# A two-layer graph network on one core: diagonal blocks written by twelve small DMAs a graph instead of one GpSimd product, and the order of steps laid out anew

## The chip, the core and the metric

The kernel runs on one core of a Trainium2 chip. Five engines work side by side, each through its own list of instructions: TensorE (PE in the profile, its weight loads PEld), VectorE (DVE), ScalarE (ACT), GpSimd (POOL) and SyncE (SP), which here only issues DMAs. They wait for one another by semaphores. The metric is the device time of one launch, in microseconds (us), lower is better.

## The reference

64 graphs of 128 nodes and 384 features, with a 128x128 adjacency matrix each. Layer 0 is masked attention with 6 heads of 64, a residual and a layer norm. Layer 1 is graph attention with 12 heads of 32:

```python
h = jnp.einsum('bnd,ade->bane', feat_in, W)
th = jnp.tanh(h)
attn_src = jnp.einsum('bane,aeo->bano', th, w_src)
attn_dst = jnp.einsum('bane,aeo->bano', th, w_dst)
attn = attn_src + jnp.swapaxes(attn_dst, 2, 3)
attn = jnp.where(attn >= 0, attn, LEAKY_ALPHA * attn)
attn = jnp.where(mask, jnp.float32(-999.0), attn)
attn = jax.nn.softmax(attn, axis=-1)
feat_out = jnp.einsum('banm,bame->bane', attn, h) + b
...
feat_out = jax.nn.elu(feat_out)
gate = jax.nn.sigmoid(feat_in @ H_w.T + H_b)
return gate * feat_out + (1.0 - gate) * feat_in
```

Then a second residual and layer norm.

## The kernel before

The 64 graphs go through in 16 groups of 4. Each engine runs the same frame (`phases`): a phase "load", a phase "first" (layer 0 of group 0), "second" (one pass of the loop order, for group 0), a loop of 13 passes, "drain" (a pass without the loads) and "last" (layer 1 of the last group). A pass of the loop order does layer 1 of group u, layer 0 of group u+1 and the transposes of x of group u+2. Inside a phase the order of every engine is a table written out by hand: `PE_LOOP`, `ACT_LOOP`, `DVE_LOOP`, `POOL_LOOP` and so on, of steps (name, graph or part). An engine works through its table in that order and waits at a step until its operands are there.

The large projections (steps v, qk, h, gate, f; line L480) are split into a high and a low part, so each is nine matmuls into one of two PSUM banks `p_bank`. Transposes and the step wb use two banks `t_bank`. A bank is free when ACT and DVE have read it.

The attention weights of layer 1 need, for each of the 12 heads, the outer combination of a value a source node and a value a destination node. The way there, for graph k of a group, is this chain:

- h (PE), th (ACT, hout), prod (POOL, L1020), sd (DVE, L895), sda (DVE, L902: a 128x24 addition in SBUF), pqw and qwhi (ACT), qwlo (DVE), qwT (PE, L610: transpose to 96 rows), qwTo (ACT, L760: copy to SBUF).
- rows (POOL, L1027): `w_rows` holds for each head n a 96x128 block in which only rows n, 32+n and 64+n are kept. It is one product of `qwT`, repeated 12 times along the free dimension, with the 0/1 mask `own_head`.
- wb (PE, L619): three matmuls of 512 columns (4 heads each) of `qwT` with `w_rows`. Then e (DVE, L924: four instructions a step) makes the weights and pv1 (PE, L630) applies them to h.

`w_rows` has two buffers, by k % 2. After pv1 come rden1, f_raw (DVE), fb (POOL), elu (ACT), ex (POOL), mixa (DVE, L942: both inputs in SBUF), mixb, sum1, stats1, mv1, rstd1, out and the store. The step x_res (POOL, L1003) adds a bias to the four graphs of x at once. In layer 0, pv0 (L564) is followed by chi (ACT) and clo (DVE), which free the operand of f.

In "first", DVE's step consts (L784 to L792) prepares small constants and waits for the last of the weight DMAs; PE's step ob multiplies two biases.

SP issues, in each pass, the load of x and adj of group u+2, and then the four stores of group u, each after its step out.

Of the kernel before, what the change touches and what calls it, by code (L numbers as in the profile page):

```python
# [1088 lines left out]
```

## Time and profile before

| what | value |
|---|---|
| time, median of 3 runs | 1256.72 us (1253.74 to 1256.73) |
| span of the profiled execution, first to last instruction | 1255.7 us |
| TensorE busy | 1134.4 us, 90% |
| VectorE busy | 1000.4 us, 80% |
| GpSimd busy | 697.6 us, 56% |
| ScalarE busy | 624.8 us, 50% |
| one pass of the loop | 75.1 us |
| mean granted TensorE clock | 0.960 of full speed |

The profiled execution has no other time than its span; the median of the runs lies 1.0 us above it. A pass of the loop repeats from pass to pass, so one is read for all. Durations of instructions that are pipelined overlap: the distance from one start to the next is what a piece takes from its engine. A busy share says how full an engine is; what a stage waits for is in the brackets of the timeline, which name the idle time before a piece and what ended it.

### The profile page before, as it was taken

Reading aid. Unit: us, or ns where it says so; the run is one execution under the profiler, and the core shown is the slowest. Engines: PE = TensorE matmul, PEld = TensorE weight load, DVE = VectorE, ACT = ScalarE, POOL = GpSimd, SP = SyncE. Lnnn points to the kernel's source line nnn. Section 1 sums busy time; section 2 is a strip of 40 time slices with the busy share of each in tenths; the row PEclk is TensorE's granted clock in tenths of the full one; section 3 lists DMA queues with packets and bytes.
Section 4 is the critical chain, followed back from the end, with each engine's and each line's share of the span. In section 5 each row is a group of like instructions: output and inputs, shape, how many; then the busy total and the mean of one; then the engine's idle time right before and its main releaser. Section 6 shows DMA issues by size and latency. Waiting matters only on the chain.

```text
span 1255.7 us, 25554 instructions
## 1 busy us (share of the span) xinstructions
PE 1134.4 (90%) x7791; PEld 1006.7 (80%) x7791; DVE 1000.4 (80%) x2384; ACT 624.8 (50%) x1996; POOL 697.6 (56%) x605
## 2 busy tenths in 40 slices
PE   6999999989899998999989899998999989899885
PEld 4888888878888887888878888887888878788774
DVE  4769789696987969788797987969788797987857
ACT  4645464454635545464554635545464554635422
POOL 0346565564655656565565655656565565656544
PEclk9998999999999999999999999999999999999975
DMA  6100010001000010010101000010010001000000
GB/s 166 29 28 8 20 29 26 27 6 28 24 19 27 13 40 6 19 33 19 27 13 39 7 19 27 13 40 6 19 33 19 27 13 40 6 19 2 26 1 26
DMA packets 34719, 30.95 MB, mean 25 GB/s; under 512 B 15872, under 2 KB 34688, under 8 KB 34688
## 3 DMA queue, kind: packets, MB, share of 16 engines
q1 hardware_dynamic: 34688, 30.57, 8.0%
q8 instruction: 16, 0.26, 0.1%
q14 instruction: 15, 0.12, 0.0%
...
## 4 chain that ended last, share of the span: by engine, by line
PE 55%; issue 16%; DVE 14%; POOL 9%; ACT 5%; DMA 0%; ACTq 0%; POOLq 0%; DVEq 0%; SPq 0%
PE p_bank L480 36%; PE context L630 7%; PE t_bank L619 4%; POOL w_rows L1027 4%; PE context L564 3%; DVE sda L902 3%; DVE weights L924 2%; POOL prod L1020 2%; PE t_bank L512 2%; PE t_bank L590 2%; POOL elu_steps L1038 1%; POOL f_b L1032 1%; ACT x1T L720 1%; DVE sd L895 1%; DVE neg_max L842 1%
## 5 line engine op out<-in xcount | busy, mean ns | idle before, releaser
L924 DVE SCALAR_TENSOR_TENSOR weights<-t_bank,pqw,clip 128x128 f32<-128x128 f32 x768 | 212.8, 341 | 33.6 <-PE t_bank L619 32.3
L1027 POOL TENSOR_TENSOR w_rows<-qwT,own_head 96x1536 fp32r<-96x1536 f32 x64 | 176.1, 2752 | 68.2 <-ACT qwT L760 68.2
L630 PEld LDWEIGHTS context<-h,weights 128*128 128x128 f32 x1536 | 197.3, 199 | 10.9 <-DVE weights L924 5.4
L630 PE MATMUL context<-h,weights 128*128 128x33 f32 x1536 | 193.0, 275 | 3.8 <-DVE weights L924 3.8
L1020 POOL TENSOR_TENSOR prod<-th,w_sd 128x768 f32<-128x768 f32 x64 | 117.6, 1838 | 132.6 <-ACT th L727 132.6
L699 ACT ACTIVATE probs<-masked,neg_max 128x128 f32<-128x128 f32 x384 | 148.8, 390 | 39.7 <-DVE neg_max L842 39.6
L1008 POOL TENSOR_TENSOR probs<-probs,rden 128x768 f32<-128x768 f32 x64 | 99.8, 1559 | 101.6 <-DVE rden L847 101.6
L480 PE MATMUL p_bank<-w_f,cT 128*128 128x384 f32 x576 | 125.8, 366 | 22.3 <-DVE cT L795 22.2
L480 PEld LDWEIGHTS p_bank<-w_f,cT 128*128 128x128 f32 x576 | 104.1, 199 | 29.4 <-DVE cT L795 29.3
L480 PE MATMUL p_bank<-w_h,x1T 128*128 128x384 f32 x576 | 117.7, 349 | 1.7 <-DVE x1T L795 1.7
L480 PE MATMUL p_bank<-w_g,x1T 128*128 128x384 f32 x576 | 117.0, 349 | 0.0
L480 PE MATMUL p_bank<-w_v,xT 128*128 128x384 f32 x576 | 116.7, 347 | 0.0
L480 PE MATMUL p_bank<-xT,w_q 128*128 128x512 f32 x432 | 112.2, 405 | 3.2 <-DVE w_k L804 3.0
L1038 POOL TENSOR_TENSOR elu_steps<-elu_steps,x 128x384 f32<-128x384 f32 x64 | 64.6, 1010 | 89.1 <-ACT elu_steps L771 89.0
L619 PE MATMUL t_bank<-w_rows,qwT 96*128 96x512 f32 x192 | 82.9, 473 | 29.6 <-POOL w_rows L1027 19.6
L480 PE MATMUL p_bank<-xT,w_k 128*128 128x512 f32 x432 | 109.0, 397 | 0.0
L480 PEld LDWEIGHTS p_bank<-w_g,x1T 128*128 128x128 f32 x576 | 104.8, 194 | 4.8 <-issue 2.6
L480 PEld LDWEIGHTS p_bank<-w_h,x1T 128*128 128x128 f32 x576 | 101.0, 193 | 2.9 <-DVE x1T L795 2.2
L480 PEld LDWEIGHTS p_bank<-w_v,xT 128*128 128x128 f32 x576 | 100.2, 190 | 1.1 <-issue 0.2
L480 PEld LDWEIGHTS p_bank<-xT,w_k 128*128 128x128 f32 x432 | 81.6, 189 | 20.0
L480 PEld LDWEIGHTS p_bank<-xT,w_q 128*128 128x128 f32 x432 | 80.8, 191 | 19.7 <-DVE w_k L804 3.4
L1032 POOL TENSOR_TENSOR f_b<-f_raw,bias 128x384 f32<-128x384 f32 x64 | 67.1, 1048 | 51.8 <-DVE f_raw L935 51.8
...
## 6 DMA issues: line engine op xcount, KB each, us to landing
...
out_dram<-y_out SPq DMA_DIRECT2D x64, 192.0 KB, 1.9
...
x<-in_L_gnn_W_dram SPq DMA_DIRECT2D x3, 192.0 KB, 6.0
```

Source lines behind the costliest of these rows:

```text
L480: last = te.matmul(dst, left(a, kt), right(b, kt), start=(n == 0), stop=(n == 3 * KT - 1))
L564: last = te.matmul(context0[b * HD0:(b + 1) * HD0, j * P:(j + 1) * P], v[:, k, n * HD0:(n + 1) * HD0], probs0T[:, k % 2, b, j * P:(j + 1) ...
L619: te.matmul(dst[:, :], qwT[:, g % 2, 0, :], w_rows[0:QW_ROWS, g % 2, heads, :].rearrange("p h i -> p (h i)"), start=True, stop=True).then_ ...
L630: last = te.matmul(context1[:, n * (HD1 + 1):(n + 1) * (HD1 + 1)], weights[:, n, :], h[:, g % 2, n, :], start=True, stop=True)
L699: last = act.activation(probs0[:, k % 2, b, j * P:(j + 1) * P], masked[:, k % 2, b * PAIRS + j, :], ACT.Exp, bias=neg_max[:, b * PAIRS + j ...
L902: dve.tensor_tensor(sda[:], sd[:], sd_shift[:], ALU.add).then_inc(s_sda, 1)
L924: last = dve.scalar_tensor_tensor(out=weights[:, n, :], in0=src[:, i * P:(i + 1) * P], scalar=pqw[:, g % 2, 0, n:n + 1], in1=clip[:, g, :] ...
L1008: pool.tensor_tensor(probs, probs, per_head(rden0[:], P), ALU.mult).then_inc(s_norm, 1)
L1020: pool.tensor_tensor(prod[:], over_heads(th[:], 2), w_sd[:], ALU.mult).then_inc(s_prod, 1)
L1027: pool.tensor_tensor(w_rows[0:QW_ROWS, k % 2], over_heads(qwT[:, k % 2, 1, :].bitcast(F32), H1), per_head(own_head[:], P), ALU.mult).then_ ...
L1032: pool.tensor_tensor(f_b[:, k % 2, :].rearrange("p (h e) -> p h e", h=H1), f_raw[:].rearrange("p (h e) -> p h e", h=H1), over_heads(bias_1 ...
L1038: pool.tensor_tensor(exp_less_x, f_exp, x1[:, k, :], ALU.subtract).then_inc(s_ex, 1)
```

## The change

The product on GpSimd, its mask and the lines that made the mask are gone. `w_rows` is set to zero once. Then SP issues for each graph twelve DMAs from SBUF to SBUF; each copies one head's three rows of 128 values from `qwT` into `w_rows`. SP's program is no longer a straight list but a table of steps like the others. PE waits for the full count of the twelve DMAs on one of two semaphores. PE's steps v and gate have each one wait more (for x's and x1's low part). All tables are written anew; a line of them stands for the rest.

```diff
-    ("prod", 0), ("x_res", 0), ("prod", 1), ("rows", 0), ("rows", 1), ("norm", 0), ("prod", 2), ("fb", 0),
...
+    ("prod", 0), ("prod", 1), ("norm", 0), ("x_res", 0), ("fb", 0), ("prod", 2), ("ex", 0), ("norm", 1), ("prod", 3),
...
+SP_LOOP = [
+    ("rows", 0), ("rows", 1), ("load", 0), ("rows", 2), ("rows", 3), ("store", 0), ("store", 1), ("store", 2),
+    ("store", 3),
+]
...
+                elif name == "rows":
+
+                    if phase == "second" and k == 0:
+                        sp.wait_ge(s_zeroed, 1)
+                        sp.sem_inc(s_rows_free, 1)
+                    sp.wait_ge(s_qwT, upto(g1, GROUP, k + 1))
+                    sp.sem_inc(s_rows_free, 1)
+
+                    wait(sp, pe["wb"], upto(g1, THIRDS * GROUP, THIRDS * (k - 1)))
+                    sp.sem_inc(s_rows_free, 1)
+                    for n in range(H1):
+                        sp.dma_start(w_rows[n:QW_ROWS:BLOCK, k % 2, n, :].bitcast(F32),
+                                     qwT[n:QW_ROWS:BLOCK, k % 2, 1, :].bitcast(F32)).then_inc(s_rows[k % 2], 16)
...
-                    te.wait_ge(s_rows, upto(g1, GROUP, g + 1))
+                    te.wait_ge(s_rows[g % 2], upto(g1, ROWS_A_GROUP, (g // 2 + 1) * ROWS_A_GRAPH))
...
-                elif name == "rows":
-                    pool.wait_ge(s_qwT, upto(g1, GROUP, k + 1))
-
-                    wait(pool, pe["wb"], upto(g1, THIRDS * GROUP, THIRDS * (k - 1)))
-                    if phase == "second" and k == 0:
-                        pool.wait_ge(s_head, 4)
-                    pool.tensor_tensor(w_rows[0:QW_ROWS, k % 2], over_heads(qwT[:, k % 2, 1, :].bitcast(F32), H1),
-                                       per_head(own_head[:], P), ALU.mult).then_inc(s_rows, 1)
```

In "first" the tables of PE and DVE now begin so:

```diff
-    ("qk", 0), ("qk", 1), ("qk", 2), ("qk", 3), ("maskT", 0), ("qk", 4), ("qk", 5), ("ob", 0), ("s", 0),
+    ("ob", 0), ("qk", 0), ("qk", 1), ("qk", 2), ("qk", 3), ("maskT", 0), ("qk", 4), ("qk", 5), ("s", 0), ("v", 0),
...
-    ("qklo", 0), ("qklo", 1), ("consts", 0), ("qklo", 2), ("qklo", 3), ("wlo", 2), ("qklo", 4), ("wlo", 3),
+    ("consts", 0), ("wlo", 2), ("qklo", 0), ("wlo", 3), ("qklo", 1), ("qklo", 2), ("clip", 0), ("qklo", 3),
```

GpSimd at the start of the loop, before. L1020 is prod, L1003 x_res, L1027 rows, L1008 norm; the lines without operands are register work.

```order
L1020 TENSOR_TENSOR prod<-th,w_sd 128x768 [waits sd_made,th_made]
L997 ISA
L360 REGISTER_ALU [waits x_loaded]
L1003 TENSOR_TENSOR x_res<-x_in,out_bias 128x1536 [waits sum0_made]
L1015 REGISTER_ALU
L1020 TENSOR_TENSOR prod<-th,w_sd 128x768 [waits sd_made,th_made]
L360 ISA [waits qwT_copied]
L1027 TENSOR_TENSOR w_rows<-qwT,own_head 96x1536 [waits pe_wb]
L1027 TENSOR_TENSOR w_rows<-qwT,own_head 96x1536 [waits pe_wb,qwT_copied]
L1006 REGISTER_ALU
L1008 TENSOR_TENSOR probs<-probs,rden 128x768 [waits rden0_made]
```

The same place now; L1025 is prod, L1013 norm, L1008 x_res, L1029 fb.

```order
L1025 TENSOR_TENSOR prod<-th,w_sd 128x768 [waits sd_made,th_made]
L1020 REGISTER_ALU
L1025 TENSOR_TENSOR prod<-th,w_sd 128x768 [waits sd_made,th_made]
L1011 ISA
L1013 TENSOR_TENSOR probs<-probs,rden 128x768 [waits rden0_made]
L1002 ISA
L1008 TENSOR_TENSOR x_res<-x_in,out_bias 128x1536 [waits sum0_made,x_loaded]
L379 REGISTER_ALU [waits f_made]
L1029 TENSOR_TENSOR f_b<-f_raw,bias 128x384 [waits mixb_made]
```

The two products w_rows have left this stretch, and x_res stands behind prod of graph 1 and norm of graph 0.

SP in the loop, before; L426 and L427 load x and adj, L433 stores.

```order
L426 ISA [waits adj_b_made,pe_xT,x_res_made]
L426 DMA x_in<-in_x_dram 128x4x384
L427 REGISTER_ALU
L427 DMA adj_in<-in_adj_dram 128x4x128
L432 ISA
L433 ISA [waits y_made]
L433 DMA out_dram<-y_out 128x384
```

SP in the loop now, up to the last of the row DMAs (L442); the four stores follow.

```order
L442 DMA w_rows<-qwT 3x128 [waits pe_wb]
L442 DMA w_rows<-qwT 3x128 x11
L436 REGISTER_ALU
L442 DMA w_rows<-qwT 3x128 [waits qwT_copied,pe_wb]
L442 DMA w_rows<-qwT 3x128 x11
L425 ISA
L429 ISA [waits adj_b_made,pe_xT,x_res_made]
L429 DMA x_in<-in_x_dram 128x4x384
L430 REGISTER_ALU
L430 DMA adj_in<-in_adj_dram 128x4x128
...
L442 DMA w_rows<-qwT 3x128 [waits pe_wb]
L442 DMA w_rows<-qwT 3x128 x11
```

The rows of graphs 0 and 1 stand ahead of the load, those of graphs 2 and 3 behind it and ahead of the stores; between the eleven DMAs of a run there is no other instruction.

PE around the transpose of graph 3 (L610 before, L619 now), before: L564 is pv0, L480 a projection, L552 pT, L630 pv1, L619 wb.

```order
L610 MATMUL t_bank<-ident,qw_parts 96x128 [waits weights_clipped,qw_lo_made]
L610 MATMUL t_bank<-ident,qw_parts 96x128
L480 MATMUL p_bank<-w_f,cT 128x384 [waits h_copied,c_lo_made]
L480 MATMUL p_bank<-w_f,cT 128x384 x8
L552 MATMUL t_bank<-ident,probs 128x128 [waits weights_clipped,probs0_normalized]
L552 MATMUL t_bank<-ident,probs 128x128 x2
L630 MATMUL context<-h,weights 128x33 [waits f_made,h_copied,weights_clipped]
L630 MATMUL context<-h,weights 128x33 x3
```

And now, from that transpose to the first wb of graph 3 (the last row); L572 is pv0, L560 pT, L639 pv1, L628 wb.

```order
L619 MATMUL t_bank<-ident,qw_parts 96x128 [waits probs0T_copied,qw_lo_made]
L572 MATMUL context<-probs0T,v 64x128 [waits c_lo_made,v_copied,probs0T_copied]
...
L560 MATMUL t_bank<-ident,probs 128x128 [waits probs0T_copied,probs0_normalized]
...
L628 MATMUL t_bank<-w_rows,qwT 128x512 [waits qwT_copied,w_rows_made0]
L628 MATMUL t_bank<-w_rows,qwT 128x512 [waits probs0T_copied,w_rows_made0]
L572 MATMUL context<-probs0T,v 64x128 [waits c_lo_made,v_copied,probs0T_copied]
...
L487 MATMUL p_bank<-w_f,cT 128x384 [waits v_copied,c_lo_made]
...
L628 MATMUL t_bank<-w_rows,qwT 128x512 [waits weights_clipped,w_rows_made0]
L639 MATMUL context<-h,weights 128x33 [waits f_made,h_copied,weights_clipped]
...
L639 MATMUL context<-h,weights 128x33 [waits f_made,h_copied,weights_clipped]
...
L628 MATMUL t_bank<-w_rows,qwT 128x512 [waits weights_clipped,w_rows_made1]
```

Between the transpose of graph 3 and its first wb stand pv0, pT, two wb of graph 2, pv0, f, a third wb and two pv1.

## Rows read from the trace of the kernel before

**Rows 1.** The page: span and busy time of each engine, its share, instructions.
```profile
span 1255.7 us, 25554 instructions
PE 1134.4 (90%) x7791; PEld 1006.7 (80%) x7791; DVE 1000.4 (80%) x2384; ACT 624.8 (50%) x1996; POOL 697.6 (56%) x605
```

**Rows 2.** Busy time by stretch: one pass, 4 us at a lower clock, the last phase.
```profile
core 0: us, PE busy (x) PEld busy (x) DVE busy (x) ACT busy (x) POOL busy (x), PEclk, DMA share, GB/s
487.80:562.90 75.10, 69.36 (x489) 61.72 (x487) 61.71 (x149) 38.48 (x126) 43.57 (x38) 0.98 0.07 22
...
570.80:574.80 4.00, 3.94 (x22) 3.18 (x22) 4.00 (x16) 0.49 (x2) 3.10 (x4) 0.62 0.00 0
...
1185.10:1255.70 70.60, 46.93 (x203) 41.74 (x200) 45.60 (x117) 15.96 (x48) 33.89 (x32) 0.68 0.05 17
```

**Rows 3.** Timeline of PE in a pass: start, duration, piece, [idle before <-releaser].
```profile
528.05 0.42 PE L610 MATMUL t_bank<-ident,qw_parts 128*96 128x128 f32 x2 [1.35 <-DVE qw_parts L795]
...
557.41 1.22 PE L542 MATMUL scores<-kT,qT 64*128 64x128 f32 x18
...
560.37 0.50 PE L619 MATMUL t_bank<-w_rows,qwT 96*128 96x512 f32 x1 [1.26 <-POOL w_rows L1027]
560.71 1.75 PE L480 MATMUL p_bank<-w_v,xT 128*128 128x384 f32 x9
562.30 0.70 PE L619 MATMUL t_bank<-w_rows,qwT 96*128 96x512 f32 x2
562.84 0.98 PE L630 MATMUL context<-h,weights 128*128 128x33 f32 x8
563.75 0.88 PE L564 MATMUL context<-probs0T,v 128*64 128x128 f32 x12
564.55 0.42 PE L610 MATMUL t_bank<-ident,qw_parts 128*96 128x128 f32 x2
564.73 1.81 PE L480 MATMUL p_bank<-w_f,cT 128*128 128x384 f32 x9
566.38 0.49 PE L552 MATMUL t_bank<-ident,probs 128*128 128x128 f32 x3
...
570.86 2.52 PE L480 MATMUL p_bank<-w_f,cT 128*128 128x384 f32 x9 [1.45 <-DVE cT L795]
```

**Rows 4.** Timeline of DVE in a pass: mixa twice, then sda.
```profile
490.80 3.03 DVE L942 SCALAR_TENSOR_TENSOR mix<-f_b,elu_steps 128x384 f32<-128x384 f32 x1
...
503.43 0.53 DVE L942 SCALAR_TENSOR_TENSOR mix<-f_b,elu_steps 128x384 f32<-128x384 f32 x1
...
524.65 2.23 DVE L902 TENSOR_TENSOR sda<-sd,sd_shift 128x24 f32<-128x24 f32 x1
```

**Rows 5.** Timeline of POOL in the same pass.
```profile
490.67 2.75 POOL L1027 TENSOR_TENSOR w_rows<-qwT,own_head 96x1536 fp32r<-96x1536 f32 x1
...
523.34 3.51 POOL L1003 TENSOR_TENSOR x_res<-x_in,out_bias 128x1536 f32<-128x1536 f32 x1
```

**Rows 6.** The SP queue at the start: issue of weight and bias DMAs.
```profile
2.32 0.86 SPq L397 DMA_DIRECT2D bias_q<-in_L_gnn_bq_dram  x1
...
16.55 0.43 SPq L412 DMA_DIRECT2D w_sd<-in_L_gnn_w_src_dram  x1
17.02 0.43 SPq L412 DMA_DIRECT2D w_sd<-in_L_gnn_w_dst_dram  x1
```

**Rows 7.** The stores' line, L433: issue times in ns, min/median/max, and landing.
```profile
L433 SPq DMA_DIRECT2D out_dram<-y_out x64: 332/333/417, 111.4 to 1253.4; - x64
...
DMA to landing us min/median/max: 1.8/1.9/2.0
```

**Rows 8.** A DMA issue of the start: size, us from issue to landing.
```profile
w_sd<-in_L_gnn_w_dst_dram SPq DMA_DIRECT2D x1, 192.0 KB, 5.4
```

**Rows 9.** Start: PE's third projection; DVE's step consts.
```profile
20.81 2.26 PE L480 MATMUL p_bank<-xT,w_q 128*128 128x512 f32 x9
...
22.43 0.55 DVE L784 TENSOR_REDUCE sd_shift<-w_sd 128x12 f32<-128x384 f32 x1
```

More of the change, by code:

```diff
@@ L62 @@
-    ("mv1", 3), ("x1", 3), ("clip", 1), ("out", 2), ("out", 3),
+    ("qklo", 0), ("x1lo", 0), ("qklo", 1), ("qklo", 2), ("sd", 0), ("sda", 0), ("gsum", 0), ("wlog", 0), ("x1lo", 1),
+    ("qwlo", 0), ("qklo", 3), ("qklo", 4), ("sd", 1), ("sda", 1), ("wlog", 1), ("qklo", 5), ("qwlo", 1), ("gsum", 1),
+    ("x1lo", 2), ("mask", 0), ("max", 0), ("e", 0), ("rden0", 0), ("e", 1), ("e", 2), ("x1lo", 3), ("gsum", 2),
+    ("e", 3), ("rden1", 0), ("f_raw", 0), ("mask", 1), ("max", 1), ("e", 4), ("sd", 2), ("e", 5), ("sda", 2),
@@ new lines @@
+    ("mixa", 0), ("wlog", 2), ("mixb", 0), ("rden0", 1), ("mask", 2), ("max", 2), ("qwlo", 2), ("sum1", 0),
+    ("stats1", 0), ("rden1", 1), ("clo", 0), ("f_raw", 1), ("sd", 3), ("sda", 3), ("rden0", 2), ("wlog", 3),
+    ("mask", 3), ("qwlo", 3), ("sum0", 0), ("max", 3), ("mixa", 1), ("clo", 1), ("mixb", 1), ("stats0", 0), ("e", 6),
+    ("mv0", 0), ("sum1", 1), ("e", 7), ("mv1", 0), ("x1", 0), ("e", 8), ("sum0", 1), ("rden0", 3), ("stats0", 1),
+    ("stats1", 1), ("e", 9), ("rden1", 2), ("f_raw", 2), ("e", 10), ("mv0", 1), ("gsum", 3), ("out", 0), ("e", 11),
@@ L63 @@
+    ("clo", 2), ("mixa", 2), ("mv1", 1), ("rden1", 3), ("clip", 0), ("x1", 1), ("f_raw", 3), ("mixb", 2), ("sum0", 2),
+    ("stats0", 2), ("out", 1), ("sum1", 2), ("mv0", 2), ("stats1", 2), ("xlo", 0), ("clo", 3), ("mv1", 2),
+    ("mixa", 3), ("xlo", 1), ("xlo", 2), ("mixb", 3), ("sum0", 3), ("stats0", 3), ("mv0", 3), ("xlo", 3), ("sum1", 3),
+    ("stats1", 3), ("mv1", 3), ("x1", 2), ("x1", 3), ("clip", 1), ("out", 2), ("out", 3),
 ]
 POOL_LOOP = [
-    ("prod", 0), ("x_res", 0), ("prod", 1), ("rows", 0), ("rows", 1), ("norm", 0), ("prod", 2), ("fb", 0),
[3 rows of a table removed]
+    ("prod", 0), ("prod", 1), ("norm", 0), ("x_res", 0), ("fb", 0), ("prod", 2), ("ex", 0), ("norm", 1), ("prod", 3),
@@ new lines @@
+    ("wlo", 4), ("qklo", 4), ("outb", 0), ("qklo", 5), ("mask", 0), ("max", 0), ("mask", 1), ("max", 1), ("rden0", 0),
+    ("mask", 2), ("max", 2), ("rden0", 1), ("mask", 3), ("glo", 0), ("max", 3), ("rden0", 2), ("clo", 0),
+    ("rden0", 3), ("sum0", 0), ("stats0", 0), ("clo", 1), ("glo", 1), ("mv0", 0), ("xlo", 0), ("clip", 1), ("clo", 2),
+    ("sum0", 1), ("stats0", 1), ("mv0", 1), ("x1", 0), ("sum0", 2), ("clo", 3), ("stats0", 2), ("xlo", 1), ("xlo", 2),
+    ("mv0", 2), ("x1", 1), ("sum0", 3), ("stats0", 3), ("mv0", 3), ("xlo", 3), ("x1", 2), ("x1", 3), ("glo", 2),
@@ L122 @@
+    ("sda", 1), ("wlog", 1), ("qwlo", 1), ("gsum", 1), ("x1lo", 3), ("e", 0), ("e", 1), ("e", 2), ("sd", 2),
+    ("rden1", 0), ("sda", 2), ("f_raw", 0), ("e", 3), ("wlog", 2), ("e", 4), ("e", 5), ("qwlo", 2), ("gsum", 2),
+    ("mixa", 0), ("mixb", 0), ("rden1", 1), ("sum1", 0), ("f_raw", 1), ("stats1", 0), ("mv1", 0), ("sd", 3),
+    ("gsum", 3), ("mixa", 1), ("sda", 3), ("wlog", 3), ("qwlo", 3), ("mixb", 1), ("sum1", 1), ("out", 0),
[3 rows of a table added]
 ]
 POOL_LAST = [
-    ("prod", 0), ("rows", 0), ("prod", 1), ("rows", 1), ("prod", 2), ("fb", 0), ("ex", 0), ("rows", 2),
@@ L128 @@
+SP_LAST = [
+    ("rows", 0), ("rows", 1), ("rows", 2), ("rows", 3), ("store", 0), ("store", 1), ("store", 2), ("store", 3),
+]
+SHIFT = {n: 2 for n in ("xT", "xhi", "xlo", "load")} | {n: 1 for n in (
+    "qk", "s", "v", "norm", "pT", "pTo", "pv0", "f", "maskT", "masks", "qkhi", "vout", "exp", "chi", "qklo", "mask",
+    "max", "rden0", "clo", "sum0", "stats0", "mv0", "x1", "clip", "x_res", "rstd0")}
 ORDERS = {
@@ L131, with phases @@
              "DVE": [("wlo", 0)] + [("xlo", g) for g in range(GROUP)] + [("wlo", 1)],
[L132 to L135 removed]
+             "POOL": [], "SP": []},
+    "first": {"PE": PE_FIRST, "ACT": ACT_FIRST, "DVE": DVE_FIRST, "POOL": POOL_FIRST, "SP": SP_FIRST},
+    "loop": {"PE": PE_LOOP, "ACT": ACT_LOOP, "DVE": DVE_LOOP, "POOL": POOL_LOOP, "SP": SP_LOOP},
+    "last": {"PE": PE_LAST, "ACT": ACT_LAST, "DVE": DVE_LAST, "POOL": POOL_LAST, "SP": SP_LAST},
 }
 ORDERS["second"] = ORDERS["loop"]
[L138 removed]
+ORDERS["drain"] = {e: [(n, k) for n, k in steps if SHIFT.get(n, 0) < 2] for e, steps in ORDERS["loop"].items()}
 BEFORE = {"first": "load", "second": "first", "loop": "second", "drain": "loop", "last": "drain"}
 WEIGHTS = ("q", "k", "v", "f", "h")
[L142 to L144 removed]
 def upto(group, per, k):
     return group * per + k
+def phases(eng, step, engine, NG):
+    for name, k in ORDERS["load"][engine]:
+        step(name, k, -2, "load")
+    for name, k in ORDERS["first"][engine]:
+        step(name, k, -1, "first")
+    for name, k in ORDERS["loop"][engine]:
+        step(name, k, 0, "second")
+    with eng.Fori(1, NG - 2) as u:
+        for name, k in ORDERS["loop"][engine]:
+            step(name, k, u, "loop")
+    for name, k in ORDERS["drain"][engine]:
+        step(name, k, NG - 2, "drain")
+    for name, k in ORDERS["last"][engine]:
+        step(name, k, NG - 1, "last")
 def bass_graph_transformer_gat(nc, x, adj, Wq, bq, Wk, bk, Wv, bv, Wf, bf, W1, b1, w_src, w_dst, H_w, H_b, out):
@@ L771, in step @@
                     act.activation(f_exp, f_neg, ACT.Exp, scale=-1.0).then_inc(s_elu, 1)
-            phases(act, step, "ACT")
+            phases(act, step, "ACT", NG)
         @block.vector
@@ L967, in step @@
                                       ALU.subtract, ALU.mult).then_inc(s_y, 1)
-            phases(dve, step, "DVE")
+            phases(dve, step, "DVE", NG)
         @block.gpsimd
```

133 lines of the change are left out of this document (50 added, 83 removed), and 58 rows, old and new, of tables (DVE_FIRST, DVE_LAST, DVE_LOOP, PE_FIRST).

## The prediction

> **What bounds the kernel now.** I read the page first: TensorE is busy 90% of the span, VectorE 80%, GpSimd 56% [rows 1]. So TensorE carries the kernel, and only its idle time and its slow time can be won. The windows say where: a pass of the loop takes 75.10 us, 69.36 of it with TensorE busy [rows 2]. So 5.74 us a pass are idle. There are 13 such passes, and the phases "second" and "drain" are nearly the same, so I count 15; what I win or lose in a pass counts 15 times.
>
> The timeline of TensorE names those gaps [rows 3]. Three are large. 1.35 us ahead of the transpose qwT of graph 0, ended by DVE's qwlo. 1.26 us ahead of the first wb of graph 2, ended by GpSimd's w_rows. 1.45 us ahead of f of graph 1, ended by DVE's clo. They sum to 4.06; the other 1.68 us are small waits for DVE.
>
> Who makes DVE late? Its timeline has mixa at 3.03 us where the same instruction takes 0.53 at another place, and an addition of 24 columns, sda, at 2.23 us [rows 4]. GpSimd's timeline gives the reason: w_rows runs from 490.67 to 493.42 and mixa ends at 493.83; x_res runs from 523.34 to 526.85 and sda ends at 526.88 [rows 5]. A DVE instruction with both inputs in SBUF stands still while a long GpSimd instruction runs. So the w_rows product costs TensorE twice: directly (1.26), and through mixa, sum0, stats0 and clo behind it on DVE's queue (1.45; the reader compares mixa at 490.80 with f one pass later at 570.86, a pass being 75.1 us). The gap of 1.35 comes from x_res, not from w_rows.
>
> There is a third cost. Behind the gap of 1.45 the nine matmuls of f take 2.52 us, where 1.81 is usual, and in the four microseconds from 570.8 the granted clock is 0.62, between the levels of 2.4 and 1.2 GHz, with TensorE just come back from that gap [rows 2, 3]. 4.0 x (1 - 0.62) = 1.5 us. In a pass 1.26 + 1.45 + 1.35 + 1.5 = 5.56 us could be won.
>
> **What is removed.** Four w_rows products a pass, 2.75 us each [rows 5]: 11 us of GpSimd's 43.57 [rows 2]. GpSimd is no bound, so they are worth what they hold up: the 1.26, and with mixa free the 1.45 and 1.5. Their other end is zero, if clo is late for another reason. I take them whole, because mixa loses 2.5 us and f waits 1.45. The tables move x_res behind prod of graph 1 and norm of graph 0. By norm, sda of graphs 0 and 1 is done, so the 1.35 goes; DVE's work beside x_res is then mostly e, mask, gsum, with an operand in PSUM. Its lower end is also zero (another two-input instruction meets x_res), worth 1.35 x 15 = 20 us.
>
> The Trainium skill (SBUF — State Buffer, Who interferes with whom) says that GpSimd and a DVE instruction with two SBUF inputs exclude each other for the whole instruction, in either order. By it sum1, mixb and sda can still meet norm or prod in the new order and lose up to such an instruction's length. I don't price it by the page; the rest below holds a term for it.
>
> **What is added.** On SP's queue 12 DMAs a graph, 48 a pass, each three rows of 512 bytes. No row shows so small a DMA, so both parts are bounded. Issue: the stores of 192 KB take 0.33 us each [rows 7]; two like DMAs back to back at the start are 0.47 apart [rows 6]; the dearest tiny one, a bias of 1.5 KB, took 0.86 [rows 6]. In the new list nothing stands between the eleven that follow each other, so I take 0.42, between 0.37 (0.33 and a gap of 0.04) and 0.47. Landing: 1.9 us for a store, 5.4 for the slowest load of the start, which shared the queues with megabytes [rows 7, 8]. I take 1.9: the queues are nearly empty in the loop (DMA share 0.07, rows 2). A graph's rows are then ready 11 x 0.42 + 1.9 = 6.5 us after qwT is copied, where the product took 2.75. The ends are 11 x 0.37 + 1.9 = 6.0 and 11 x 0.90 + 5.4 = 15.3.
>
> The Trainium skill (DMA: Bandwidth & Descriptors, Rules for kernel authors) speaks against such transfers: coalesce, since below 64 KB one pays mostly overhead. Here the overhead is paid in latency on a queue with nothing else to do, and what it costs depends on the work that TensorE has meanwhile.
>
> **What hides it.** From qwT of graph 3 to its first wb TensorE now has pv0 0.80, pT 0.33, two wb 0.54, pv0 0.80, f 1.65, wb 0.27 and two pv1 at 0.91: 6.2 us, by distances of starts [rows 3]. It needs the transpose 0.2, ACT's copy, which I estimate at 0.5 with its wait, and then 6.5: 7.2. It waits 1.0. For graph 2: s 1.22, four pT 1.3, v 1.6, f 1.65, qwT 0.2, pv0 0.8, 6.8 us against 7.1: it waits 0.3. For graph 0: two qk, x1T, gate, qwT, s, v, over 9 us: nothing. For graph 1 SP is still issuing graph 0 when qwT arrives, but wb stands behind s, v, h, gate and two pv1: nothing. The load is queued behind rows 1 and waits for x_res, while rows 2 stands behind it; x_res, by my count of the tables, is done well ahead of qwT of graph 2 (two norm, fb and ex lie between on GpSimd). The stores stand behind rows 3, and out of graph 0 comes later than that on DVE. So 1.3 us new waits a pass. I add 0.6 for what becomes late next: DVE, whose work of some 57 us (61.7 less the 4.6 that mixa and sda stood still) is packed in the second half of the pass, where clo, xlo and clip free operands and banks for f and xT. Sum: 5.56 - 1.3 - 0.6 = 3.66 a pass, 15 x 3.66 = 55 us.
>
> **Start and end.** In "first", DVE begins with consts, which needs the last weight DMA: issued at 17.02, landed 5.4 later at 22.4 [rows 6, 8]. Then come consts, four small instructions of which the first takes 0.55 [rows 9], wlo (three times as wide as a sum of 384) and only then qklo 0, at about 25 by my estimate, which frees the bank for PE's third projection. That began at 20.81 before [rows 9]. So it is late by some 5 us, less about 2 for ob (six matmuls), which PE now does ahead of it; with wlo between the qklo I take +4 (0 to 6). "last" is a chain through one group, 70.6 us with TensorE busy 46.9 [rows 2]: each graph gets its rows 3.8 us later (6.5 for 2.75), but no product blocks DVE there and gate and h of graph 3 stand earlier. I take 0, from -5 to +8. Clearing w_rows costs GpSimd a few microseconds at a time when it has nothing to do: 0.
>
> Sum: the span of 1255.7 less 55 plus 4 is 1204.7; runs lie 1.0 above it: 1206.
>
> **Rivals.**
> 1. The DMA queue becomes the pace. The gain of 5.56 less 0.6 is used up when the new waits reach 5, that is when rows arrive 1.85 us later for both graph 2 and 3 (2 x 1.85 + 1.3 = 5): R = 8.35, an issue distance of 0.59 in place of 0.42. The 0.86 of the tiny bias speaks for it, the 0.33 of the stores against. At 0.75, graph 3 waits 4.7, graph 2 3.9 and graph 0 about 1, 9.6 in all: 5.56 - 0.6 - 9.6 = -4.6, 15 times 70 us: 1330. At 0.65 it is 1275 to 1280, which I take as its time.
> 2. The clock falls again. If waits of 1.0 and 0.3 us and small ones around them lie close, TensorE may come back at the lower clock as after the 1.45 gap, and 1.5 us a pass stay lost, perhaps with 0.3 more of waits: 27 us less gain, 1233. For it: the gap of 1.45 did it. Against: the 1.26 gap did not.
> 3. The new order hides everything: rows at 6.0, no new wait, and some of the small 1.68 goes too: 5.56 + 0.5, 15 x 6.06 = 91: 1171. Against it: DVE is 82% busy a pass.
> 4. Nothing comes of it: DVE's waits take the place of those removed (clo is late by its own queue), 1254 to 1257.
>
> **How the numbers follow.** Forecast 0.50 (1190 to 1222), clock 0.16 (1222 to 1250), all hidden 0.13 (1165 to 1190), nothing 0.06, slower 0.15. The range from 1172 to 1250 holds about 0.8; both ends of the landing above 1.9 lie outside it, in the slow rival. Faster or slower is told from no change at 0.3%, 3.8 us: faster 0.79, same 0.06, slower 0.15.
>
> **What would show it.** Right: passes of 71 to 72 us; no DVE mixa of 3 us and sda at 0.2; row DMAs 0.4 apart, landed 6 to 7 us after the copy; TensorE waiting for DMA ahead of the first wb of graph 3 by about 1 us and of graph 2 by less; granted clock 0.99 in the pass; its third projection at 25 to 26 us. Wrong: row DMAs 0.6 or more apart, or landing well above 1.9; a slow stretch behind the new wait; mixb, sum1 or sda of 1.5 us and more beside norm or prod.

## The result and the profile after

The changed kernel takes 1478.37 us (median of 4 runs, 1477.54 to 1480.51) against 1255.95 us for the kernel before (4 runs, 1253.74 to 1256.73): a ratio of 1.178, 95% interval 1.176 to 1.180. It is 222 us slower, where 1206 was forecast. The first rival, the DMA queue as the pace, was the right mechanism, but even its dearest case (1330) was 150 us short.

The page of the changed kernel, in the form of [rows 1], and under it the chain that ended last, by engine:

```profile
span 1478.7 us, 26562 instructions
...
PE 1307.9 (88%) x7791; PEld 1157.0 (78%) x7791; DVE 946.7 (64%) x2384; ACT 617.2 (42%) x1996; POOL 508.5 (34%) x538
...
PE 53%; SPq 33%; issue 5%; DMA 4%; ACT 2%; DVE 2%; ACTq 0%; POOL 0%; POOLq 0%; DVEq 0%
```

GpSimd lost 189 us of work and DVE 54, as meant. TensorE still executes 7791 matmuls but is busy 174 us longer. And a third of the chain is SPq, SyncE's queue of DMA issues, from an engine that computes nothing.

Where the 223 us of span went, by the starts of the last maskT transpose of each pass and of the first v of "second":

| stretch | before, us | after, us | difference |
|---|---|---|---|
| up to "second" | 60.1 | 69.8 | +9.7 |
| "second" | 76.7 | 90.2 | +13.5 |
| loop, 13 passes | 976.2 (75.1 each) | 1151.2 (88.55 each) | +175.0 |
| "drain" | 72.0 | 86.2 | +14.1 |
| "last" | 70.7 | 81.3 | +10.7 |

So the pass is what must be explained. The windows view has one whole pass and three stretches in it, and "last", with the columns of [rows 2]:

```profile
601.10:689.80 88.70, 81.00 (x488) 72.04 (x487) 58.37 (x149) 37.92 (x124) 31.55 (x33) 0.85 0.06 19
636.00:644.00 8.00, 7.94 (x43) 7.54 (x43) 5.49 (x13) 3.17 (x11) 3.81 (x3) 0.57 0.38 107
661.00:666.00 5.00, 4.76 (x21) 3.78 (x22) 3.15 (x12) 0.35 (x2) 1.84 (x4) 0.50 0.01 2
670.00:684.00 14.00, 14.00 (x58) 13.39 (x58) 8.26 (x27) 1.14 (x2) 5.36 (x8) 0.51 0.04 14
1397.30:1478.70 81.40, 47.10 (x204) 40.64 (x202) 41.48 (x115) 16.27 (x48) 20.30 (x24) 0.65 0.05 16
```

TensorE is idle 88.70 - 81.00 = 7.7 us a pass, against 75.10 - 69.36 = 5.7 before [rows 2]. That is only 2.0 us of the 13.6. The granted clock gives the rest: 0.85 in place of 0.98. In three stretches it is 0.50 to 0.57, so near the lower of its two levels, 1.2 GHz. They lose 8 x 0.43 + 5 x 0.50 + 14 x 0.49 = 12.8 us, where the pass before lost 75.1 x 0.02 = 1.5.

TensorE's timeline of this pass says what stands ahead of each slow stretch; these rows answer to [rows 3]:

```profile
627.53 0.50 PE L628 MATMUL t_bank<-w_rows,qwT 96*128 96x512 f32 x1 [0.73 <-DMA w_rows<-qwT]
...
636.06 0.63 PE L628 MATMUL t_bank<-w_rows,qwT 96*128 96x512 f32 x1 [2.41 <-DMA w_rows<-qwT]
...
641.40 2.52 PE L487 MATMUL p_bank<-w_h,x1T 128*128 128x384 f32 x9
...
661.24 1.22 PE L628 MATMUL t_bank<-w_rows,qwT 96*128 96x512 f32 x2 [2.86 <-DMA w_rows<-qwT]
...
663.87 3.25 PE L487 MATMUL p_bank<-w_f,cT 128*128 128x384 f32 x9
...
669.73 0.50 PE L628 MATMUL t_bank<-w_rows,qwT 96*128 96x512 f32 x1 [0.67 <-DMA w_rows<-qwT]
...
671.90 3.08 PE L487 MATMUL p_bank<-w_g,x1T 128*128 128x384 f32 x9
...
675.44 5.28 PE L639 MATMUL context<-h,weights 128*128 128x33 f32 x24
680.52 3.23 PE L487 MATMUL p_bank<-w_f,cT 128*128 128x384 f32 x9
```

Each of the four graphs has one wait for the row DMAs: 0.73, 2.41, 2.86 and 0.67 us, 6.7 in all. Behind the second, third and fourth the same nine matmuls take 2.52 to 3.25 us, where 1.81 is usual [rows 3]; 24 matmuls of pv1 take 5.28. The fourth wait is short because TensorE came to it late: the rows landed at 669.7 after an unbroken row of issues, and TensorE had run from 661 to 666 at a clock of 0.50.

Now the chain of waits through the same pass (start, duration, what):

```profile
617.64 0.39 ACT qwT L769
618.06 0.06 issue
618.27 0.70 SPq L442
619.02 0.64 SPq L442
...
626.76 0.65 SPq L442
...
633.62 0.64 SPq L442
634.30 1.64 DMA w_rows<-qwT
635.94 0.12 issue
636.06 0.63 PE t_bank L628
```

From qwT of graph 0 the chain runs through 24 issues in a row, those of graph 0 and then those of graph 1: 16.0 us to the start of the last one, then 1.64 from there to its landing. From 651.96 to 669.73 it does so again for graphs 2 and 3. Together that is 35.6 of 88.7 us in which nothing but this queue sets the time. The source view of L442 has the issue's length (minimum, median, maximum in ns) and who waited:

```profile
L442 SPq DMA_DIRECT2D w_rows<-qwT x768: 639/640/841, 86.6 to 1456.6; - x192
...
  PE t_bank L628: 108.0, 63
```

Last, the rows that answer to [rows 4, 9]: DVE's sda and mixa in the same pass, and TensorE's ob, its third projection and s at the start.

```profile
614.19 0.18 DVE L911 TENSOR_TENSOR sda<-sd,sd_shift 128x24 f32<-128x24 f32 x1
...
647.00 0.55 DVE L951 SCALAR_TENSOR_TENSOR mix<-f_b,elu_steps 128x384 f32<-128x384 f32 x1
```

```profile
14.40 4.19 PE L501 MATMUL context<-probs,bias_v 128*128 128x384 f32 x6 [2.74 <-DMA bias_f<-in_L_gnn_bf_dram]
...
25.84 3.65 PE L487 MATMUL p_bank<-xT,w_q 128*128 128x512 f32 x9 [3.04 <-DVE qT L832]
...
37.56 1.22 PE L550 MATMUL scores<-kT,qT 64*128 64x128 f32 x18 [1.56 <-DVE kT L832]
```

DVE no longer stands still: 0.18 and 0.55 in place of 2.23 and 3.03. None of the 64 sda takes more than 0.19 us, and none of the 64 mixa, mixb or sum1 more than 0.56.

### The profile page after: what moved, and what is told of

Same layout as the page of the kernel before. It is cut to its first block, busy times and chain, and to the rows that moved or that the text cites. A ratio compares the mean times of both kernels' runs of the same rounds, so it can differ in the third digit from the quotient of the medians.

```text
span 1478.7 us, 26562 instructions
## 1 busy us (share of the span) xinstructions
PE 1307.9 (88%) x7791; PEld 1157.0 (78%) x7791; DVE 946.7 (64%) x2384; ACT 617.2 (42%) x1996; POOL 508.5 (34%) x538
## 4 chain that ended last, share of the span: by engine, by line
PE 53%; SPq 33%; issue 5%; DMA 4%; ACT 2%; DVE 2%; ACTq 0%; POOL 0%; POOLq 0%; DVEq 0%
SPq L442 32%; PE p_bank L487 30%; PE context L639 11%; PE scores L550 4%; DMA w_rows<-qwT 4%; PE t_bank L628 3%; PE t_bank L560 2%; PE context L572 1%; PE t_bank L519 1%; PE t_bank L598 1%; ACT qwT L769 1%; ACT elu_steps L776 1%; DVE xT L804 1%; PE t_bank L619 1%; ACT xT L677 0%
## 5 line engine op out<-in xcount | busy, mean ns | idle before, releaser
L639 PEld LDWEIGHTS context<-h,weights 128*128 128x128 f32 x1536 | 244.4, 242 | 9.3 <-DVE weights L933 5.5
L639 PE MATMUL context<-h,weights 128*128 128x33 f32 x1536 | 238.4, 316 | 3.6 <-DVE weights L933 3.6
L628 PE MATMUL t_bank<-w_rows,qwT 96*128 96x512 f32 x192 | 108.8, 586 | 109.4 <-DMA w_rows<-qwT 108.0
L1013 POOL TENSOR_TENSOR probs<-probs,rden 128x768 f32<-128x768 f32 x64 | 94.1, 1470 | 283.1 <-DVE rden L856 283.1
L1025 POOL TENSOR_TENSOR prod<-th,w_sd 128x768 f32<-128x768 f32 x64 | 119.0, 1859 | 203.8 <-ACT th L736 203.8
L487 PE MATMUL p_bank<-w_f,cT 128*128 128x384 f32 x576 | 158.1, 435 | 2.9 <-DVE cT L804 1.8
L628 PEld LDWEIGHTS t_bank<-w_rows,qwT 96*128 96x128 f32 x192 | 47.4, 259 | 123.7 <-DMA w_rows<-qwT 87.7
L487 PEld LDWEIGHTS p_bank<-w_f,cT 128*128 128x128 f32 x576 | 133.9, 253 | 11.4 <-DVE cT L804 6.4
L487 PE MATMUL p_bank<-w_g,x1T 128*128 128x384 f32 x576 | 134.8, 387 | 0.2 <-DVE gate_sum L898 0.2
L717 ACT ACTIVATE probs0T<-t_bank 128x384 f32<-128x384 f32 x128 | 58.7, 483 | 176.0 <-PE t_bank L560 175.6
L1029 POOL TENSOR_TENSOR f_b<-f_raw,bias 128x384 f32<-128x384 f32 x64 | 68.2, 1066 | 155.6 <-DVE f_raw L944 155.6
L832 DVE SCALAR_TENSOR_TENSOR qT<-p_bank,bias_q,qT 128x512 fp32r<-128x512 f32 x48 | 36.0, 751 | 104.9 <-ACT qT L691 104.9
L994 POOL TENSOR_TENSOR ve<-mv,eps 128x1 f32<-128x1 f32 x128 | 33.7, 263 | 201.9 <-DVE mv L874 125.9
```

Of the source, the lines that this page charges most:

```text
L487: last = te.matmul(dst, left(a, kt), right(b, kt), start=(n == 0), stop=(n == 3 * KT - 1))
L628: te.matmul(dst[:, :], qwT[:, g % 2, 0, :], w_rows[0:QW_ROWS, g % 2, heads, :].rearrange("p h i -> p (h i)"), start=True, stop=True).then_ ...
L639: last = te.matmul(context1[:, n * (HD1 + 1):(n + 1) * (HD1 + 1)], weights[:, n, :], h[:, g % 2, n, :], start=True, stop=True)
L717: act.activation(probs0T[:, g % 2, b, :], t_bank[t_at("pT", k, phase)][:, 0:PAIRS * P], ACT.Copy).then_inc(s_pT, 1)
L832: dve.scalar_tensor_tensor(out=dst[:, LO, k // 2, :], in0=p_bank[p_at("qk", k, phase)][:, :], scalar=bias_q[:, k % 2, k // 2:k // 2 + 1], ...
L1013: pool.tensor_tensor(probs, probs, per_head(rden0[:], P), ALU.mult).then_inc(s_norm, 1)
```

## The experiments

The theory after this reading: SP's queue, one issue every 0.68 us with two graphs back to back, makes TensorE wait, and the waits lower its clock, which costs more than they do. The rival: the new order of steps is the slow part and the DMAs are nearly hidden.

**The two halves of the change apart.** First the new tables with the product back on GpSimd, its four steps put in by hand:

```diff
-    ("prod", 0), ("prod", 1), ("norm", 0), ("x_res", 0), ...
-    ("fb", 1), ("norm", 2), ("ex", 1), ("rstd0", 0), ...
+    ("prod", 0), ("prod", 1), ("rows", 0), ("rows", 1), ("norm", 0), ("x_res", 0), ...
+    ("fb", 1), ("rows", 2), ("norm", 2), ("ex", 1), ("rows", 3), ("rstd0", 0), ...
```

> The new tables, but w_rows by the one product on GpSimd as before (rows 0 and 1 set behind prod 1, rows 2 ahead of norm 2, rows 3 behind ex 1, the last phase's GpSimd table as before); nothing is left out. Theory (the row DMAs alone cost the time, the order is sound): a pass of about 73 to 75 us, no stretch at half clock, time 1235 to 1260. Rival (the new order is itself bad, for instance DVE is packed too late): a pass of 80 us or more, time above 1320, with TensorE waiting for DVE's weights, cT or xT and not for w_rows.

1378.16 us (1367.76 to 1402.61), a ratio of 1.093 (1.087 to 1.099). The time lies above the theory's range and within the rival's, but the reason is not quite the rival's. The new tables have no room for a product of 2.75 us: norm of graph 2 stands behind rows 2, and TensorE waits 2 us for it, then 1.47 for clo, with a pv0 of 1.55 us where 0.88 is usual:

```profile
443.92 0.54 PE L546 MATMUL t_bank<-ident,probs 128*128 128x128 f32 x3 [2.01 <-POOL probs L1003]
...
449.49 1.55 PE L558 MATMUL context<-probs0T,v 128*64 128x128 f32 x12 [1.47 <-DVE cT L790]
```

A pass takes 81.6 us on average, at a clock of 0.89. TensorE's idle time, 5.4 us a pass, is no longer than before (5.7); it is the clock that makes the pass longer. So the sum of the waits does not tell what the clock will do. Some of this is my placing of the product, so this run does not price the tables. Then the other half, the twelve DMAs under the old tables (those of before without GpSimd's rows, SP's as changed):

> The old tables of PE, ACT, DVE and GpSimd (rows taken out of GpSimd's), with the twelve DMAs a graph from SP; nothing is left out. Theory (rows come 9.3 us after the copy, 0.69 us for each issue and 1.65 for landing, and TensorE's cover decides): before the first wb of graph 2 TensorE has only some 2.7 us of work and before that of graph 3 some 4, so it waits 6 to 7 us twice a pass and the lower clock follows each wait: a pass of 95 to 105 us, time 1550 to 1680. Rival (the order decides, the DMAs are mostly hidden): at or below the changed kernel's 1478.

1686.63 us (one run), 7 us above the range: the cost of the DMAs without an order that makes room for them. A pass takes 102.4 us, and its four waits for rows are 3.70, 4.44, 7.31 and 5.42 us. The last two:

```profile
636.26 0.79 PE L636 MATMUL t_bank<-w_rows,qwT 96*128 96x512 f32 x1 [7.31 <-DMA w_rows<-qwT]
...
654.34 1.22 PE L636 MATMUL t_bank<-w_rows,qwT 96*128 96x512 f32 x2 [5.42 <-DMA w_rows<-qwT]
```

So with the DMAs the new tables are worth some 208 us, and the rival of the slow order falls. TensorE is idle 22.7 us of a pass here, at a clock of 0.83, little below the 0.85 of the changed kernel with its 7.7 us idle.

**Half the DMAs.** All tables as changed; heads 6 to 11 get no rows, so what is computed for them is wrong, at the same work for the other engines.

```diff
-    ROWS_A_GRAPH = 16 * H1
+    ROWS_A_GRAPH = 16 * (H1 // 2)
-                    for n in range(H1):
+                    for n in range(H1 // 2):
```

> The changed kernel with row DMAs for heads 0 to 5 only; the rows of heads 6 to 11 stay zero, so their weights are not what the reference has. Same instructions on all other engines. Theory: rows come 5 x 0.69 + 1.65 = 5.1 us after the copy, ahead of every wb (6 us of work or more), so no wait for DMA, no clock loss, and the order shows its own worth: a pass of 69 to 72 us, time 1170 to 1210. Rival A (it is landing, or the DMAs' traffic on SBUF, that slows the pass): waits for w_rows stay above 1 us each and the time above 1350. Rival B (DVE takes the place of the wait): a pass of 74 to 76 us, 1250.

1258.09 us (1250.52 to 1270.41), a ratio of 1.005 (1.001 to 1.009). The waits for DMA are gone altogether with the issue as long as before, 0.64 us. So 220 us hang on the row DMAs of which half are gone; that it is their number and not their bytes is shown further down, where 32 times the bytes run faster. But the time only comes back to that of before, where 1170 to 1210 was expected; rival B, DVE in the place of the wait, had said 1250. Two passes that follow each other, and the largest wait left:

```profile
363.98:436.64 72.66, 70.16 (x488) 62.50 (x486) 57.65 (x149) 38.05 (x124) 31.50 (x33) 0.98 0.07 23
436.64:510.71 74.07, 71.83 (x488) 63.92 (x486) 57.65 (x149) 38.15 (x124) 31.51 (x33) 0.95 0.07 23
```

```profile
497.26 0.28 PE L590 MATMUL t_bank<-ident_b,adj_b 128*128 128x128 bf16 x2 [0.97 <-DVE weights L933]
```

A pass averages 73.8 us, only 1.3 less than before, though idle time fell from 5.7 to 2.4: about every other pass runs at a mean clock of 0.95, and one of the 13 at 0.87. With rows that nobody waits for the change would have gained 1.3 us a pass, not the 5 that I had counted. Even that is the upper end: the trace is of the shortest of the eight runs (1250.52), and the median is 7.6 us longer, some 0.5 us a pass.

**The clock.** Useless transposes of the identity ahead of the first wb of each graph, in the bank that wb then overwrites, so that TensorE works instead of waiting:

```diff
+FILL = {0: 6, 3: 20, 6: 24, 9: 20}
...
-                    te.wait_ge(s_rows[g % 2], ...)
                     dst = bank(t_bank, t_freed, name, k, g1, phase)
+                    for _ in range(FILL.get(k, 0)):
+                        te.transpose(dst[:, 0:P], ident[:], ident[:])
+                    te.wait_ge(s_rows[g % 2], ...)
```

> The changed kernel with transposes of the identity into the bank of wb put ahead of its wait, 6, 20, 24 and 20 of them at wb 0, 3, 6 and 9, 0.11 us each: 0.7, 2.2, 2.6 and 2.2 us of work that nobody uses, 7.7 us a pass; the output is unchanged. Theory (some 12 of the 13.6 us a pass are the lower clock, which follows TensorE's idle time): the waits turn into work, the granted clock of the pass rises from 0.85 to 0.97 or more and the pass falls from 88.7 to 77 to 80 us, time 1300 to 1350. Rival (the clock goes with something else, such as the DMAs themselves or the total load): the clock stays near 0.85 and the time at 1478 or, with the added work, up to 1550.

1366.92 us (1361.70 to 1372.38), a ratio to before of 1.087 (1.083 to 1.092): 111 us faster than the changed kernel, by adding work, though 17 us above the range that was expected. A pass of it, two of its fillers and the waits behind them:

```profile
429.17:508.80 79.63, 76.88 (x559) 68.59 (x558) 57.94 (x148) 38.07 (x124) 31.69 (x33) 1.00 0.07 22
```

```profile
448.82 2.78 PE L628 MATMUL t_bank<-ident 128*128 128x128 f32 x24
451.84 0.74 PE L631 MATMUL t_bank<-w_rows,qwT 96*128 96x512 f32 x2 [0.24 <-DMA w_rows<-qwT]
...
456.93 2.38 PE L628 MATMUL t_bank<-ident 128*128 128x128 f32 x20
460.32 0.50 PE L631 MATMUL t_bank<-w_rows,qwT 96*128 96x512 f32 x1 [1.02 <-DMA w_rows<-qwT]
```

The clock is 1.00 in this pass. Over all 13 passes it is 0.98, as in the kernel before, against 0.85 in the changed kernel, and a pass takes 80.9 us on average. The DMAs are the same, so the rival, that the clock goes with them, falls. That splits the 13.5 us: 88.55 - 80.9 = 7.7 are the clock that the waits cost, 80.9 - 73.8 = 7.1 are the queue itself (filled or waited, it is the same time), and 73.8 - 75.1 = -1.3 is what the rest of the change gains. The split is not pure. At the full clock TensorE comes to its waits sooner, so part of the 12.8 us turns into waiting. The fillers take 8.4 us a pass where 6.7 were waited. And the kernel with six DMAs loses more to the clock (0.96 over the loop) than the filled one or the one before (0.98).

**Why 0.64 us.** First, each DMA with all 96 rows instead of three, same count, still SBUF to SBUF:

```diff
-                        sp.dma_start(w_rows[n:QW_ROWS:BLOCK, k % 2, n, :].bitcast(F32),
-                                     qwT[n:QW_ROWS:BLOCK, k % 2, 1, :].bitcast(F32))
+                        sp.dma_start(w_rows[0:QW_ROWS, k % 2, n, :].bitcast(F32),
+                                     qwT[0:QW_ROWS, k % 2, 1, :].bitcast(F32))
```

> The changed kernel with each row DMA made 96 rows of 512 bytes in place of 3 (48 KB in place of 1.5 KB), same count, queue and direction; the blocks then hold all heads' rows, so the weights are not the reference's. Theory (the 0.64 us of issue belong to a DMA over 3 rows: SP itself has to make up the 13 of 16 increments that no DMA engine makes): issue falls to 0.33 to 0.45 us as with the stores, rows are complete 6 to 7 us after the copy, waits for w_rows fall below 1 us, a pass of 73 to 77 us, time 1250 to 1310, although 32 times the bytes move. Rival A (0.64 belongs to a DMA from SBUF to SBUF): issue stays at 0.64, time at 1478 or above. Rival B (the bytes bound it): issue 1 us or more, time above 1500.

```profile
L442 SPq DMA_DIRECT2D w_rows<-qwT x768: 511/595/1717, 84.8 to 1375.4; - x192
...
  PE t_bank L628: 83.7, 50
```

1402.34 us (1400.25 to 1404.44), in none of the three ranges. Moving 32 times the bytes is 76 us faster. 24 issues take 15.4 us in place of 16.7: the smaller DMA is the dearer one, but by a little. So the theory that the 0.64 us belong to a DMA of three rows finds little support: with 96 rows it is 0.60, where 0.33 to 0.45 was expected. With issues 1.3 us shorter for a pair of graphs the waits for rows sum to 83.7 us in place of 108.0, and the loop's clock is 0.89 in place of 0.85. Second, the three rows read from x in HBM:

```diff
-                        sp.dma_start(w_rows[n:QW_ROWS:BLOCK, k % 2, n, :].bitcast(F32),
-                                     qwT[n:QW_ROWS:BLOCK, k % 2, 1, :].bitcast(F32))
+                        sp.dma_start(from_x[n:QW_ROWS:BLOCK, k % 2, :],
+                                     x_dram[n:QW_ROWS:BLOCK, 0, 0:P])
```

> The changed kernel, but the twelve DMAs of a graph read their three rows of 512 bytes from x in HBM and write a buffer that nobody uses; w_rows stays zero. Number, size, order and waits are the same. Theory A: the 0.64 us of an issue come from the direction, SBUF to SBUF. Then an issue falls to 0.33 to 0.42 as in the loads and stores [rows 6, 7], 24 of them are issued in about 10 us, and the time falls to 1290 to 1350. Theory B: the 0.64 come from the small strided access itself or its count of rows. Then the issues stay 0.64 long and 0.68 apart, 24 take 16.7 us, and the time stays 1450 to 1490.

```profile
L443 SPq DMA_DIRECT2D from_x<-in_x_dram x768: 650/651/847, 86.0 to 1463.6; - x192
```

1492.68 us (1487.53 to 1497.83), theory B, by 3 us above its range. The direction is not the reason: 0.65 us from HBM as well. What in the access makes an issue cost 0.64 where a store takes 0.33 [rows 7] stays open: 3 rows and 96 rows both cost about twice the store's 128 rows of 1.5 KB. The number of rows alone, or their stride of 32, does not explain it. Whether issuing half of the DMAs from another engine would help was not tried.

**The start.** The changed kernel with the old tables of "first":

> The changed kernel with the first phase's tables of the kernel before (ob behind qk 5, DVE's consts behind qklo 1). Theory: the 9.7 us that the start lost come from DVE waiting in consts for the last weight DMA: the second phase begins at 60 us again and the time falls by 8 to 11 us to 1467 to 1470. Rival (clearing w_rows on GpSimd or the wait on x's low part costs it): it begins at 65 us or later.

1471.92 us (one run), 2 us above the range. "second" begins at 60.65 us in place of 69.77, so 9.1 us of the 9.7 at the start belong to the new tables of "first". Which step in them did it, this run does not tell, since it puts back all of them.

**DVE's two stalls, in the kernel before.** Can the gain that was forecast be had without any DMA? Two moves, each by itself and then both:

```diff
-    ("prod", 0), ("x_res", 0), ("prod", 1), ("rows", 0), ("rows", 1), ("norm", 0), ...
+    ("prod", 0), ("prod", 1), ("rows", 0), ("rows", 1), ("x_res", 0), ("norm", 0), ...
```

> The kernel before with one step moved: GpSimd's x_res of the loop stands behind rows 1 and ahead of norm 0, in place of behind prod 0; nothing is left out. Theory (sda stands still while x_res runs, and TensorE waits 1.35 us a pass for it): sda of graph 0 takes 0.2 us, the 1.35 goes, and nothing replaces it (norm 0 comes 1 us later): 15 x 1.3 = 20 us, time 1233 to 1240. Rival (the wait only moves, to norm or to the next two-input instruction): within 4 us of 1256.

1228.53 us (1226.25 to 1231.40), a ratio of 0.979 (0.976 to 0.981), pass 73.0: more than expected. The other:

```diff
-    ("max", 3), ("mixa", 1), ("sum0", 0), ("mixb", 1), ("stats0", 0), ("clo", 1), ("mv0", 0), ("sum1", 1),
+    ("max", 3), ("sum0", 0), ("stats0", 0), ("clo", 1), ("mv0", 0), ("mixa", 1), ("mixb", 1), ("sum1", 1),
```

> The kernel before, with DVE's mixa of graph 1 moved behind sum0 0, stats0 0, clo 1 and mv0 0, and x_res left where it was. Theory: the two stalls are separate, so mixa's own part is worth the wait of 1.45 us at f of graph 1 and its slow stretch, 20 to 25 us of the whole: 1232 to 1240, with the 1.35 at qwT of graph 0 still there. Rival: the stalls hang together (as moving x_res took the 1.26 at wb too): alone it brings 10 us or less, 1246 to 1257.

1225.28 us (1223.97 to 1227.32), a ratio of 0.976 (0.973 to 0.978), pass 73.0: again more than expected, and the stalls are separate. The two traces hold each other's control. With x_res moved, DVE's sda and mixa read:

```profile
438.02 0.18 DVE L902 TENSOR_TENSOR sda<-sd,sd_shift 128x24 f32<-128x24 f32 x1
...
477.89 3.03 DVE L942 SCALAR_TENSOR_TENSOR mix<-f_b,elu_steps 128x384 f32<-128x384 f32 x1
```

With mixa moved:

```profile
436.24 2.23 DVE L902 TENSOR_TENSOR sda<-sd,sd_shift 128x24 f32<-128x24 f32 x1
...
481.25 0.52 DVE L942 SCALAR_TENSOR_TENSOR mix<-f_b,elu_steps 128x384 f32<-128x384 f32 x1
```

Each move removes its own stall and leaves the other. The Trainium skill (SBUF — State Buffer, Who interferes with whom) says that a DVE instruction with two SBUF inputs contends with a GpSimd instruction that reads SBUF, by an exclusive lock. These two traces agree for DVE as the one that waits, with 3.03 against 0.52 (0.76 at most in that run) and 2.23 against 0.18. Both moves together:

> The same, and DVE's mixa 1 moved behind sum0 0, stats0 0, clo 1 and mv0 0; nothing is left out. Theory (w_rows 3 holds mixa 1 for 2.5 us, DVE's queue holds clo 1, TensorE waits 1.45 us for f 1 and runs 4 us at a lower clock after it): 1.3 + 1.45 + 1.5 = 4.2 us a pass, granted clock of a pass from 0.98 to 1.00, time 1190 to 1200. Rival (DVE is the bound there, another wait takes its place): 1225 to 1240, no better than with x_res alone.

1207.52 us (1205.89 to 1209.19), a ratio of 0.961 (0.958 to 0.963): faster than both kernels by a table edit of two steps, though 7.5 us above the range that was expected. A pass takes 71.9 us on average. The windows have a pass, and in it a stretch that is slow again:

```profile
489.29:561.96 72.67, 70.51 (x488) 63.57 (x487) 58.27 (x149) 38.60 (x124) 43.89 (x37) 0.95 0.07 23
532.00:539.50 7.50, 7.50 (x47) 6.79 (x46) 6.15 (x13) 4.04 (x16) 6.46 (x6) 0.54 0.00 0
```

Ahead of it stand waits of only 0.23 and 0.44 us. I tried to fill the second with a pT that stood behind it:

```diff
-    ("s", 2), ("qwT", 2), ("pT", 2), ("pv0", 0), ...
+    ("s", 2), ("pT", 2), ("qwT", 2), ("pv0", 0), ...
```

> The kernel with x_res and mixa moved, and in TensorE's loop order also pT 2 ahead of qwT 2, where a wait of 0.44 us for qwlo stood and a slow stretch of about 7 us followed it. Theory: the work of 0.33 us fills most of the wait, and the stretch behind it runs at the full clock: 2 to 3 us a pass, 1170 to 1190. Rival: the stretch comes whatever stands there (the wait of 0.23 ahead of it suffices), only 0.3 us a pass are won: 1200 to 1206.

1207.10 us (1205.77 to 1208.35): no change. pT has a wait of its own there, for GpSimd's norm, and the slow stretch comes after all:

```profile
533.51 0.59 PE L552 MATMUL t_bank<-ident,probs 128*128 128x128 f32 x3 [0.41 <-POOL probs L1008]
...
539.17 2.45 PE L480 MATMUL p_bank<-w_v,xT 128*128 128x384 f32 x9
```

The wait was replaced, not filled. But the slow stretch does not come in every pass. Of the 13 passes of this run five take 72.6 us at a clock of 0.95 and five 71.0 us at 1.00, with the same small waits. So they can bring it and need not. Where it stays away, another wait stands further on:

```profile
466.89 0.50 PE L619 MATMUL t_bank<-w_rows,qwT 96*128 96x512 f32 x1 [1.22 <-POOL w_rows L1027]
```

That is the wait for the product [rows 3]; in the slow passes it is absent, since TensorE comes later. So the stretch costs 1.6 us where it comes, and I have no version without it. (The expectation of the run with mixa alone took the move of x_res to have removed this wait. That held for the passes that are slow ahead of it, not for the others.)

## Why the prediction was wrong

- **Issue distance, the step that failed first.** I took 0.42 us from the stores and two loads, between 0.37 and 0.47, and kept 0.90 as an outer end. It is 0.68 to 0.69. Rows of graph 0 are complete 11 x 0.69 + 1.64 = 9.2 us after the first issue, which starts 0.2 us after their copy, not 6.5. The landing, 1.9 forecast, was 1.64. None of the rows that I went by was a DMA of this shape. The nearest in size were the three biases of 1.5 KB at the start. I quoted one, at 0.86 [rows 6], as the dearest and gave it to the rival; the same queue has the others at 0.49 and 1.06. The measured 0.64 lies among these three and not with the stores. (The 5.4 us that I called the slowest landing of the start was not that either: weights took up to 7.4. Nothing in the sum hung on it. Two sums were off by little: graph 2 needs 7.2 us as graph 3 does, not 7.1, and at a distance of 0.65 the rival's own sum gives 1282, not 1275 to 1280.)
- **The queue behind the queue.** "For graph 1 SP is still issuing graph 0 when qwT arrives ... nothing" was wrong, and it holds for graph 3 behind graph 2 as well. A second graph's rows come 23 distances and a landing after the first issue of the pair, 17.7 us by the trace. Graph 1, priced at nothing, has a wait of 2.41. For graph 3 I let the rows start at its own copy; they start when graph 2's last issue is out. I asked what is queued behind what for the load and the stores but not for the rows themselves.
- **The clock, the largest term by size.** I priced it at up to 1.5 us a pass, the loss that the trace showed after one wait of 1.45. The changed pass loses 12.8 by the windows, and 7.7 by the filled kernel. The rows of before had shown one slow stretch of 4 us; I took its length as fixed. After waits of 2.41 and 2.86 the stretches are 8 and 5 us, and the last is 14 us behind a wait of 0.67 that followed 3 us after a slow stretch. What sets their length stays open. Rival 1 carried no clock term at all, which is why its 1330 was short: at 0.69 its own sum gives about 1300, and 15 times the 11.3 us of clock by the windows (12.8 less 1.5) bring it to about 1470.
- **What is removed: right as a mechanism, too large as a sum.** mixa and sda run at 0.55 and 0.18, and the waits at f and at the first qwT are gone. Nor did sum1, mixb or sda meet norm or prod at a cost. But 5.56 less 0.6 a pass was counted, and the kernel with six DMAs, which waits for no rows, gained 1.3 at most. In the kernel before, the two moves gained 2.1 each and 3.2 together, where I had 1.35 and 2.95. In the kernel with six DMAs idle time fell by 3.3 us a pass and busy time grew by 1.6, since a slow stretch came back, behind a largest wait of 0.97. What failed is the assumption that the clock stays full once the large waits are gone.
- **Start: +4 forecast (0 to 6), +9.7 measured.** The third projection came at 25.84, as said (25 to 26). The credit of 2 us for ob, now ahead, was used up between that projection and s: the projection takes 3.65 in place of 2.26, and s waits 1.56 for DVE. So s starts 6.1 us later than before, and 3.6 more are lost on the way to "second".
- **"last": 0 forecast (-5 to +8), +10.7 measured.** The 48 issues stand there in two rows of 24, within 44.4 us, and the waits for rows sum to 7.4 us. I had counted 3.8 us for a graph and hidden it.
- **Loads and stores** were no trouble, as said.
- **The chances.** Slower had 0.15. Of the three DMAs in the trace as small as the new ones two cost 0.86 and 1.06 and one 0.49, the cheap ones were over 100 times larger, and the rival decided from 0.59 on. The rival belonged near one in two.
